# Where layer two's softmax denominators are summed: a stage of their own, or inside pass two

## The chip, the cores and the metric

The program runs on one core of a Trainium2 chip. The metric is the device time of the slowest (here the only) core, in microseconds. The kernel before takes 3942.93 us, the median of 3 runs (3939.38 to 3952.08).

## What is computed

A graph of 3125 nodes with 256 features and 103,125 edges (50,000 drawn ones in both directions and one loop per node, sorted by destination) goes through two layers. The first is attention with 8 heads, then a projection and a two-layer MLP with norms. The second, which this change touches, is

```python
z = proj_s[src] + proj_t[dst]
z = jnp.where(z >= 0, z, NEG_SLOPE * z)
e = (z @ W_attn.T)[:, 0]
m = jax.ops.segment_max(e, src, num_segments=n)
e_exp = jnp.exp(e - m[src])
denom = jax.ops.segment_sum(e_exp, src, num_segments=n)
alpha = e_exp / denom[src]
msg = feature[src] * alpha[:, None]
agg = jax.ops.segment_sum(msg, dst, num_segments=n)
return agg @ W_fc.T + b_fc
```

The maximum is taken by source node and the denominator is summed by source node, while the edges lie in order of destination. All scores here lie within 60 of each other, so one shift common to all edges does instead of one per node; a slow path behind a test holds for other data, and isn't taken.

## The kernel before

Edges lie in tiles of 128 (one edge per partition); there are 806 tiles (`T`), and a visit takes `G` = 30 of them, so that 27 visits walk over all. Each pass over the edges is a loop over the visits, written out separately for each engine, with semaphores between the engines.

- Pass one is the attention of layer one. GpSimd gathers the rows of the source nodes by index (line 779, two gathers of 128 rows for each of the 15 pairs of tiles), TensorE expands the rows of the destination nodes with one-hots (line 900), VectorE multiplies and reduces, TensorE sums by node (line 913).
- A stage by nodes (projection, MLP, norms) writes `proj_rows`, `narrow_rows` and `part_rows` to DRAM.
- Pass two computes the scores `e`. For each pair p of a visit, GpSimd gathers `proj_rows` or `narrow_rows` into the one slot of that pair, as soon as VectorE has read the pair of the visit before (`slots_free[1]`) and the indices are there (`idx_in[1]`). TensorE expands the pair into `px` (line 900; it runs up to 3 pairs ahead), VectorE adds both (`rows`, line 1615) and takes the dot product with the attention vector (`attend`, lines 1620 and 1622). At the visit's end three small instructions (lines 1633, 1635, 1638) put 30 columns of scores into `e_all`. ScalarE makes the one-hots of the destination nodes for the visit to come (lines 1142, 1147). SyncE sends the gathered features on to `x_edges` in the order of the edges (lines 545, 546) and loads indices and one-hot sources.
- After pass two come the range of the scores (lines 1646 to 1656), one exponential over `e_all` on ScalarE (line 1286), and then the denominators: `e_exp` is split into three bf16 parts (lines 1702, 1705), and for each of 26 blocks of `DT` = 31 tiles VectorE builds one-hots of the high part of the source (`src` // 128, 25 values; line 1715) and of its low part (`src` % 128; line 1716), multiplies the high ones by the three parts (line 1719), and TensorE runs 31 matmuls of 75 columns that add into `pn` (line 1045). Low and high one-hots are double-buffered. VectorE then sums the three parts (line 1722), takes reciprocals (lines 1725 to 1736), scales the node features by them (line 1743, 5 pieces), and SyncE writes these as `feat_rows` (line 725).
- Before line 1698 VectorE waits for `x1_back`, one load of all node features (line 684). SyncE holds the loads of low parts (line 691), of the streams `x_edges` (line 687) and of the first output row back until `recip2`, the last step of the reciprocals.
- Pass three gathers `feat_rows` (GpSimd waits for all of `feat_stored`), weighs them by `e_exp` and the looked-up reciprocals, and sums by destination node.

## Time and profile before

| | us |
|---|---|
| median of 3 runs | 3942.93 |
| span of the profiled execution | 3995.8 |
| pass one | about 150 to 1560 |
| stage by nodes | about 1560 to 1910 |
| pass two | 1907 (first gather) to 3173.7 (last scores) |
| range and exponential | 3173.7 to 3183.9 |
| denominators | 3183.9 to 3309 |
| scaled features, first loads | 3309 to 3333 |
| pass three | 3333 to 3996 |

The profile is one execution; of its own time only the span, from the first to the last instruction, is recorded, and it lies 52.9 us above the median of the runs. How to read it: the page gives the busy share of each engine over the whole span, and 40 slices of it. A table by stretch gives the same for parts. Groups put instructions of one line and shape together with their mean duration and with the engine's idle time just before them, and name what ended that idle time. The timeline shows single instructions.

### The profile page before, as it was taken

What the parts mean: (1) busy time and instruction counts of PE and PEld (TensorE: products, weight loads), DVE (VectorE), ACT (ScalarE), POOL (GpSimd) and SP (SyncE); (2) the same over time, 40 slices, a digit from 0 to 9 for tenths busy, and PEclk for the clock granted to TensorE, in tenths of its full rate; (3) what the DMA queues carried; (4) which work ended last, traced back from release to release, by engine and by line L of the source; (5) the groups of instructions that cost most, each with busy time, mean ns of one, the idle gap of its engine ahead of it and who ended that gap; (6) DMA issues with size and microseconds to landing.
All of it is one profiled execution on the core that took longest, in us unless ns stands there. A gap on an engine that the chain in (4) does not pass through costs nothing.

```text
span 3995.8 us, 54572 instructions
## 1 busy us (share of the span) xinstructions
PE 2303.1 (58%) x11454; PEld 1677.2 (42%) x11455; DVE 2175.4 (54%) x6197; ACT 1124.8 (28%) x2699; POOL 1960.5 (49%) x1970
## 2 busy tenths in 40 slices
PE   4456666666666664878233333333334395777776
PEld 2244444444444443756122222222122294656655
DVE  5455655556555564242344444444444596677676
ACT  0144554445544553333111111111112100111111
POOL 0255555555555553121566666666656303544443
PEclk9788877788778877988666666667666656988898
DMA  4666656666666663121677777777767505666564
GB/s 141 195 179 178 182 176 180 175 180 181 177 178 176 176 177 100 50 86 47 191 215 221 212 211 214 211 214 228 210 206 216 175 0 186 205 197 204 183 208 150
DMA packets 365707, 698.62 MB, mean 175 GB/s; under 512 B 77317, under 2 KB 247039, under 8 KB 365674
## 3 DMA queue, kind: packets, MB, share of 16 engines
q0 software_dynamic: 134784, 425.63, 36.1%
q1 hardware_dynamic: 220602, 256.40, 20.6%
q10 hardware_dynamic: 10288, 16.23, 1.1%
q8 instruction: 10, 0.16, 0.0%
q14 instruction: 23, 0.19, 0.0%
HBM read 597.23 MB, written 100.85 MB: 175 GB/s over the span
## 4 chain that ended last, share of the span: by engine, by line
another core or an unknown queue 27%; PE 26%; DVE 24%; issue 16%; DMA 3%; DVEq 2%; SPq 1%; POOL 1%; ACT 1%; ACTq 0%; POOLq 0%
PE ps_px L900 7%; DVE sb_prod L1622 4%; DVE sb_wide L1615 4%; DVE sb_score L1468 4%; PE ps_pa L913 3%; PE ps_px L913 2%; PE ps_px L998 2%; PE ps_px L1007 2%; PE ps_pa L1058 2%; PE ps_pn L1045 2%; DVE sb_wide L1477 1%; PE ps_px L876 1%; DVE sb_parts L1814 1%; DVE sb_prod L1462 1%
## 5 line engine op out<-in xcount | busy, mean ns | idle before, releaser
L900 PE MATMUL ps_px<-sb_parts 128*128 x2430 | 468.2, 358 | 798.8 <-DVE sb_wide L1615 563.1
L900 PEld LDWEIGHTS ps_px<-sb_parts 128*128 128x128 bf16 x2430 | 268.1, 122 | 999.4 <-DVE sb_wide L1615 625.6
L779 POOL DMA_INDIRECT sb_ring<-kv_rows,sb_idx x324 | 322.5, 995 | 357.8 <-DVE sb_wide L1477 152.6
L913 PE MATMUL ps_pa<-sb_wide,sb_onehot 128*128 128x264 f32 x864 | 302.8, 483 | 317.1 <-DVE sb_wide L1477 256.2
L779 POOL DMA_INDIRECT sb_ring<-proj_rows,sb_idx x324 | 316.5, 977 | 303.8 <-issue 170.8
L779 POOL DMA_INDIRECT sb_parts<-kv_rows,sb_idx x324 | 316.0, 975 | 206.9 <-DVE sb_wide L1477 107.4
L1142 ACT ACTIVATE sb_parts<-sb_bits,sb_nn_tab 128x768 bf16<-128x768 int16 x135 | 126.3, 937 | 1016.6 <-remote 606.9
L900 PE MATMUL ps_px<-sb_parts,sb_xwm 128*128 x2430 | 397.9, 309 | 19.2 <-ACT sb_xwm L1147 14.6
L779 POOL DMA_INDIRECT sb_w<-narrow_rows,sb_idx x324 | 315.3, 973 | 163.7 <-issue 102.2
L913 PE MATMUL ps_px<-sb_wide,sb_onehot 128*128 128x264 f32 x756 | 252.9, 466 | 197.3 <-DVE sb_wide L1477 124.3
L779 POOL DMA_INDIRECT sb_w<-feat_rows,sb_idx x162 | 158.9, 981 | 416.0 <-issue 192.3
L913 PEld LDWEIGHTS ps_pa<-sb_wide,sb_onehot 128*128 128x128 f32 x864 | 187.2, 239 | 371.1 <-DVE sb_wide L1477 258.6
L900 PEld LDWEIGHTS ps_px<-sb_parts,sb_xwm 128*128 128x128 bf16 x2430 | 270.6, 111 | 149.3 <-issue 51.1
L1622 DVE SCALAR_TENSOR_TENSOR sb_prod<-sb_wide,sb_attn_hi 128x256 f32<-128x256 f32 x810 | 310.5, 422 | 0.0
L1161 ACT ACTIVATE sb_onehot<-sb_bits 128x256 f32<-128x256 bf16 x405 | 166.3, 411 | 469.8 <-remote 316.7
L1154 ACT ACTIVATE sb_bits<-sb_iota_w,sb_ndst_f 128x128 bf16<-128x128 f32 x810 | 278.8, 391 | 40.7 <-issue 28.2
L1615 DVE TENSOR_TENSOR sb_wide<-ps_px,sb_ring 128x516 f32<-128x516 f32 x162 | 111.2, 694 | 303.0 <-remote 221.7
L1468 DVE TENSOR_REDUCE sb_score<-sb_prod 128x16 f32<-128x512 f32 x405 | 273.8, 676 | 0.0
L913 PEld LDWEIGHTS ps_px<-sb_wide,sb_onehot 128*128 128x128 f32 x756 | 156.9, 228 | 242.1 <-DVE sb_wide L1477 115.1
L1615 DVE TENSOR_TENSOR sb_wide<-ps_px,sb_w 128x516 f32<-128x516 f32 x162 | 112.2, 693 | 237.2 <-remote 190.4
L1462 DVE TENSOR_TENSOR sb_prod<-ps_px,sb_ring 128x512 f32<-128x512 f32 x162 | 111.1, 686 | 232.0 <-remote 138.4
L1814 DVE TENSOR_SCALAR sb_parts<-sb_iota_n,sb_dst_g,sb_ex_g 128x128 f32<-128x128 f32 x810 | 218.4, 361 | 35.0 <-issue 33.7
(256 smaller groups left out, 4473.2 us busy)
## 6 DMA issues: line engine op xcount, KB each, us to landing
sb_bits<-dst_short SPq DMA_DIRECT2D x280, 192.0 KB
x_edges<-sb_ring SPq DMA_DIRECT2D x54, 768.0 KB
sb_slots<-x_edges SPq DMA_DIRECT2D x54, 768.0 KB
x_edges<-sb_slots SPq DMA_DIRECT2D x27, 768.0 KB
sb_w<-x_edges SPq DMA_DIRECT2D x27, 768.0 KB
sb_msg<-lo_rows SPq DMA_DIRECT2D x28, 576.0 KB
kv_rows<-sb_slots ACTq DMA_DIRECT2D x25, 256.0 KB, 2.8
sb_parts<-part_rows SPq DMA_DIRECT2D x28, 193.5 KB
```

What stands on the lines that cost most here:

```text
L779: pool.indirect_dma_start(out=out[:, i, :], out_offset=None, in_=rows, in_offset=bass.IndirectOffsetOnAxis(ap=idx[:, 2 * p + i:2 * p + i + ...
L900: mm = pe.matmul(into, hots_t[L][:, 2 * p + i, :], flat(visit_parts[:, bass.ds(parity, 1), a, 0:width]), start=(a == 0), stop=(a == 2))
L913: mm = pe.matmul(into[:, 0:C + H], onehot[:, j, :], sums_in[:, 2 * (p % FLIGHT) + i, :], start=(p % EARLY == 0 and i == 0), stop=True, ski ...
L998: mm = pe.matmul(px[:, 2 * (s % 2) + f // 4, (f % 4) * P:(f % 4 + 1) * P], w1[:, c, f * P:(f + 1) * P], tr[:, s, c, :], start=(c == 0), st ...
L1142: act.activation(hots_t[L][:, half(h), :], drow[:, h], ACT.Abs, bias=nn_tab[:, bass.ds(v, 1)]).then_inc(far[L], 1)
L1154: ins = act.activation(away[:, j, :], iota_w[:], ACT.Abs, bias=ndst_f[:, bass.ds(t0 + (2 * p + i), 1)])
L1161: act.activation(onehot[:, places(p), :], away[:, places(p), :], ACT.Relu, bias=1.0, scale=-1.0).then_inc(hot[0], 1)
L1462: dve.tensor_tensor(prod[:, p % 3].rearrange("p (j c) -> p j c", j=2), px[:, p % FLIGHT, :].rearrange("p (j c) -> p j c", j=2), kv_pairs[p ...
L1468: dve.tensor_reduce(score[:, p % FLIGHT], prod[:, p % 3].rearrange("p (j h d) -> p j h d", j=2, h=H), AX, ALU.add).then_inc(red1, 1)
L1615: dve.tensor_tensor(zbuf[:, pair(p), :], px[:, places(p), 0:CW], proj_slots(p)[:, :, 0:CW], ALU.add).then_inc(slots_free[1], 1)
L1622: ins = dve.scalar_tensor_tensor(out=prod[:, p % 3, i * C:i * C + C], in0=zbuf[:, 2 * (p % FLIGHT) + i, 0:C], scalar=0.0, in1=attn_hi[:], ...
L1814: ins = dve.tensor_scalar(weights[:, j, :], iota_n[:], dst_g[:, j:j + 1], ex_g[:, j:j + 1], ALU.is_equal, ALU.mult)
```

## The change

The denominators move into pass two. The exponential used for them is shifted not by the maximum over all edges but by the largest score of the first visit, which is found once, in the second visit. For each visit v, its 30 columns are handled during visit v+1: ScalarE takes the exponential of the 30 columns, VectorE splits it into three bf16 parts, makes the low one-hots of 30 tiles with one comparison (3840 columns), the high ones with one (750), and the product with the three parts (2250); TensorE runs 30 matmuls of 75 columns, 6 behind each of the pairs 10 to 14. The buffers are single now. The visit's last columns follow after the loop. The exponential over `e_all` stays (pass three needs it). The feature load comes back in 5 pieces, each waited for by the piece that it feeds; the loads of low parts and of the first output row don't wait any more, the streams wait for `den0`, and the scaled features come behind the first one-hots of pass three. The slow path sums its denominators by itself.

```diff
+            def top_transposed():
+                pe.wait_ge(shift_set, 1)
+                pe.transpose(pa[0:1, 0:P], top[:, 0:1], ident[:]).then_inc(shift_pe, 1)
...
+            def denominators(v, g):
+                if g == 0:
+                    pe.wait_ge(dv, v + 1)
+                for j in range(g * R, (g + 1) * R):
+                    mm = pe.matmul(pn[:, 0:3 * W], lo_hot[:, :, j], hi_ex[:, :, :, j].rearrange("p a n -> p (a n)"),
+                                   start=False, stop=True, skip_group_check=True)
+                mm.then_inc(dpe, 1)
...
+            def scored(v, earlier=None, second=False):
                 parity = visit_value(pe, "parity", v)
                 for p in range(PAIRS):
                     expand(1, CW, parity, v, p)
+                    if second and p == 2:
+                        top_transposed()
+                    if second and p == 4:
+                        top_spread()
+                    if earlier is not None and p >= PAIRS - HALVES:
+                        denominators(earlier, p - (PAIRS - HALVES))
...
+            def score_exps(v):
+                act.wait_ge(zs, v * len(ZS) + ZS["masked"])
+                act.wait_ge(shift_set, 3)
+                act.activation(ex_v, dots[:, 2], ACT.Exp, bias=shift[:, 0:1]).then_inc(den_ex, 1)
+
+            node_half(0)
+            with act.Fori(0, total - 1) as u:
+                node_half(act.snap(u + 1))
+                score_exps(u)
+            score_exps(last_visit(act))
...
+            dve.wait_ge(part_out, 2 * (W // NB) * 16 + 1)
+            dve.tensor_copy(low_iota, iota_b[:].unsqueeze(2).broadcast_to([P, P, G]))
+            dve.tensor_copy(iota_j, iota_b[:, 0:W].unsqueeze(2).broadcast_to([P, W, G])).then_inc(fv, 1)
...
+                if step == "high":
+                    dve.tensor_tensor(hi_hot, iota_j, src_hib[:, bass.ds(t0, G)].unsqueeze(1).broadcast_to([P, W, G]), ALU.is_equal).then_inc(dh, 1)
...
+                if step == "ex":
+                    dve.wait_ge(den_ex, v + 1)
+                    dve.tensor_tensor(left0, ex_v, kept, ALU.mult).then_inc(dsplit, 1)
...
+                if step == "low":
+                    t0 = visit_value(dve, "tile", v)
+                    dve.wait_ge(dpe, v * HALVES + HALVES)
+                    dve.tensor_tensor(lo_hot, low_iota, src_lob[:, bass.ds(t0, G)].unsqueeze(1).broadcast_to([P, P, G]), ALU.is_equal)
+                if step == "spread":
+                    done("part2")
+                    dve.wait_ge(dh, v + 1)
+                    dve.tensor_tensor(hi_ex, hi_hot.unsqueeze(1).broadcast_to([P, 3, W, G]),
+                                      ex_parts.unsqueeze(2).broadcast_to([P, 3, W, G]), ALU.mult).then_inc(dv, 1)
+
+            WEIGHED = {1: ["low"], 3: ["ex"], 4: ["part0"], 5: ["left1"], 6: ["part1", "high"], 7: ["left2", "part2", "spread"]}
...
+                    if earlier is not None:
+                        for step in WEIGHED.get(p, []):
+                            weighed(earlier, step)
...
+                dve.tensor_copy(kept, low_dots[:, 1]).then_inc(zs, 1)
...
-            dve.wait_ge(ea, 1)
-            dve.wait_ge(x1_back, 16)
-
-            dve.tensor_copy(iota_j, iota_b[:].unsqueeze(2).broadcast_to([P, P, DT])).then_inc(fv, 1)
...
-            with dve.Fori(0, TD // DT // 2) as it:
-                for b in range(2):
...
-                    dve.tensor_tensor(hi_hot[:, b], iota_j[:, 0:W], src_hib[:, bass.ds(t0, DT)].unsqueeze(1).broadcast_to([P, W, DT]), ALU.is_equal).then_inc(dh, 1)
-                    dve.tensor_tensor(lo_hot[:, b], iota_j, src_lob[:, bass.ds(t0, DT)].unsqueeze(1).broadcast_to([P, P, DT]), ALU.is_equal)
...
+            for step in ("low", "high", "ex", "part0", "left1", "part1", "left2", "part2", "spread"):
+                weighed(last, step)
...
             for c in (0, 1):
                 indices(tile, c)
-            sp.wait_ge(fv, FVS["recip2"])
             low_rows(tile)
+            features(0)
+            sp.wait_ge(fv, FVS["den0"])
             for c in range(THIRDS):
                 stream(tile, c)
-            features(0)
```

## Rows read from the trace of the kernel before

**Rows 1.** The page: span, busy time and share of each engine
```profile
span 3995.8 us, 54572 instructions
PE 2303.1 (58%) x11454; PEld 1677.2 (42%) x11455; DVE 2175.4 (54%) x6197; ACT 1124.8 (28%) x2699; POOL 1960.5 (49%) x1970
```

**Rows 2.** Table by stretch: bounds and length in us, then busy time per engine
```profile
core 0: us, PE busy (x) PEld busy (x) DVE busy (x) ACT busy (x) POOL busy (x), PEclk, DMA share, GB/s
150.00:1560.00 1410.00, 885.29 (x4252) 652.26 (x4253) 813.83 (x1803) 696.13 (x1970) 798.49 (x810) 0.80 0.61 177
1910.00:3152.00 1242.00, 456.78 (x2358) 260.86 (x2358) 560.39 (x2418) 218.33 (x261) 784.84 (x809) 0.63 0.71 214
3184.00:3309.00 125.00, 109.91 (x806) 105.83 (x806) 113.83 (x93) 0.00 (x0) 0.00 (x0) 0.50 0.00 0
```

**Rows 3.** Groups, 3183.5 to 3309 us: busy, mean ns, idle before, releaser
```profile
L1045 PE MATMUL ps_pn<-sb_parts 128*128 128x75 bf16 x806 | 109.9, 311 | 17.0 <-DVE sb_parts L1719 17.0
L1716 DVE TENSOR_TENSOR sb_parts<-sb_parts,sb_src_lob 128x3968 bf16<-128x3968 bf16 x26 | 59.4, 2286 | 0.0
L1719 DVE TENSOR_TENSOR sb_parts<-sb_parts,sb_msg 128x2325 bf16<-128x2325 bf16 x26 | 36.5, 1405 | 0.0
L1715 DVE TENSOR_TENSOR sb_parts<-sb_parts,sb_src_hib 128x775 bf16<-128x775 bf16 x26 | 15.0, 578 | 6.3 <-PE ps_pn L1045 5.8 <-DVEq L1708 0.5
```

**Rows 4.** Timeline, end of pass two: start, duration, engine, line, [idle before <-releaser]
```profile
3171.54 0.39 SPq L684 DMA_DIRECT2D sb_ring<-proj_rows  x1
...
3173.54 0.19 DVE L1638 TENSOR_TENSOR sb_e_all<-sb_e_all,sb_dots 128x30 f32 x1
...
3178.29 1.04 ACT L1286 ACTIVATE sb_e_all<-sb_e_all,sb_shift 128x896 f32<-128x896 f32 x1 [33.60 <-DVEq L1692]
...
3183.86 2.23 DVE L1698 COPY sb_parts<-sb_iota_b 128x3968 bf16<-128x3968 bf16 x1 [6.33 <-DMA sb_ring<-proj_rows]
```

**Rows 5.** Timeline, from the denominators to the first gather of pass three
```profile
3309.22 0.19 DVE L1740 COPY sb_hn<-sb_iota_b 128x75 bf16<-128x75 bf16 x1
...
3309.32 7.09 DVE L1743 TENSOR_TENSOR sb_ring<-sb_ring,sb_denom 128x1280 f32<-128x1280 f32 x5
...
3316.73 0.82 DVE L1749 TENSOR_SCALAR sb_bits<-sb_msg,sb_hn 128x2304 bf16<-128x2304 bf16 x1
3317.48 1.70 DVE L1756 TENSOR_TENSOR sb_bits<-sb_hn,sb_src_hib 128x450 bf16<-128x450 bf16 x3
...
3318.47 6.62 SPq L725 DMA_DIRECT2D feat_rows<-sb_ring  x5
...
3333.11 1.19 POOL L779 DMA_INDIRECT sb_w<-feat_rows,sb_idx  x1 [156.00 <-issue]
```

**Rows 6.** Gathers of line 779, two groups: min/median/max ns, first and last start
```profile
L779 POOL DMA_INDIRECT sb_slots<-kv_rows,sb_idx x162: 943/949/1286, 167.7 to 1515.1; - x162
L779 POOL DMA_INDIRECT sb_slots<-proj_rows,sb_idx x162: 945/949/1190, 1938.4 to 3148.9; - x162
```

**Rows 7.** Timeline of VectorE inside one visit of pass two
```profile
2523.60 0.70 DVE L1615 TENSOR_TENSOR sb_wide<-ps_px,sb_ring 128x516 f32<-128x516 f32 x1 [6.66 <-remote]
...
2536.28 0.70 DVE L1615 TENSOR_TENSOR sb_wide<-ps_px,sb_w 128x516 f32<-128x516 f32 x1 [11.23 <-remote]
```

**Rows 8.** Timeline of TensorE in the same visit
```profile
2516.24 0.84 PE L900 MATMUL ps_px<-sb_parts 128*128 x6 [0.53 <-issue]
...
2524.35 1.48 PE L900 MATMUL ps_px<-sb_parts 128*128 x6 [7.28 <-DVE sb_wide L1615]
```

**Rows 9.** Timeline of GpSimd in the same visit, its two long waits
```profile
2510.66 0.94 POOL L779 DMA_INDIRECT sb_ring<-proj_rows,sb_idx  x1 [5.90 <-DVE sb_wide L1615]
...
2537.79 0.94 POOL L779 DMA_INDIRECT sb_w<-narrow_rows,sb_idx  x1 [4.76 <-DVE sb_wide L1615]
```

**Rows 10.** Timeline, pass three: a gather and the VectorE instructions beside it
```profile
3396.25 2.01 POOL L779 DMA_INDIRECT sb_w<-feat_rows,sb_idx  x1 [0.30 <-issue]
```

**Rows 11.** Timeline of VectorE in the stretch of rows 10
```profile
3395.73 1.71 DVE L1756 TENSOR_TENSOR sb_bits<-sb_hn,sb_src_hib 128x450 bf16<-128x450 bf16 x3
```

More of the change, by code:

```diff
@@ L331, in build @@
         x_in = [sem(f"x_in{c}") for c in range(THIRDS)]
-        x1_back = sem("x1_back")
+        x1_back = [sem(f"x1_back{i}") for i in range(NB)]
+        shift_pe = sem("shift_pe")
+        shift_set = sem("shift_set")
+        den_ex = sem("den_ex")
         lo_in = sem("lo_in")
@@ L466, in build @@
         SPLITS = 5
+        ZS = steps(["dots", "low", "masked", "kept", "added"])
+        DS = steps(["ex", "part0", "left1", "part1", "left2", "part2"])
         feats = ring
@@ L683, in _ @@
             sp.sem_inc(sp_seen, 1)
-            sp.dma_start(x1, proj_rows[:, CW:ROW].rearrange("(w p) c -> p w c", p=P)).then_inc(x1_back, 16)
+            for i in range(NB):
+                some = slice(i * W // NB, (i + 1) * W // NB)
+                sp.dma_start(x1[:, some], proj_rows[i * W // NB * P:(i + 1) * W // NB * P, CW:ROW].rearrange("(w p) c -> p w c", p=P)).then_inc(x1_back[i], 16)
             def stream(tile, c):
@@ L1643, in _ @@
+            scored(0)
+            scored(1, 0, second=True)
+            with dve.Fori(0, total - 2) as u:
+                scored(dve.snap(u + 2), dve.snap(u + 1))
             for c in range(THIRDS):
@@ L1654, in _ @@
             dve.tensor_scalar(slow_i[:], dots[0:1, 1, 0:1], SPREAD, None, ALU.is_gt).then_inc(ev, 1)
-            dve.tensor_scalar(shift[:], rng_all[:, 0:1], -1.0, None, ALU.mult).then_inc(ev, 1)
-            dve.wait_ge(ev, 5)
+            dve.wait_ge(ev, 4)
+            dve.wait_ge(fv, FVS["dsum"])
             dve.sem_inc(slow_flag, 1)
@@ L1740, in _ @@
             dve.tensor_copy(hi_iota, iota_b[:, 0:W].unsqueeze(1).broadcast_to([P, 3, W])).then_inc(fv, 1)
-            for i in range(NB):
-                some = slice(i * W // NB, (i + 1) * W // NB)
-                dve.tensor_tensor(feats[:, some, :], x1[:, some, :], denom[:, 2, some].unsqueeze(2).broadcast_to([P, W // NB, C]), ALU.mult).then_inc(fv, 1)
             dve.wait_ge(fv, FVS["hi"])
+            dve.wait_ge(ea, 1)
             def low_onehots(v):
@@ L1837, in _ @@
             high_onehots(0)
+            for i in range(NB):
+                some = slice(i * W // NB, (i + 1) * W // NB)
+                dve.wait_ge(x1_back[i], 16)
+                dve.tensor_tensor(feats[:, some, :], x1[:, some, :], denom[:, 2, some].unsqueeze(2).broadcast_to([P, W // NB, C]), ALU.mult).then_inc(fv, 1)
             reciprocals(0)
```

173 lines of the change are left out of this document (106 added, 67 removed).

## The prediction

> **What bounds the kernel now.** I read the page first for the shares. No engine is over 58% busy [rows 1], so no engine bounds the whole, and each stage has to be read by itself. The table by stretch comes next, for the three stages that matter [rows 2]. In 3184 to 3309 TensorE is busy 109.9 of 125 us and VectorE 113.8, while GpSimd and the DMA stand still: a stage of engine work and nothing else. The groups of that stretch show its beat: per block of 31 tiles VectorE needs 0.58 + 2.29 + 1.41 = 4.27 us (lines 1715, 1716, 1719), and TensorE's 806 matmuls (26 blocks) are busy 109.9 us, 4.2 us per block [rows 3]. The two take turns with two buffers and cost about 4.7 us per block, 122 us for 26.
>
> Pass two, where this work is to go, is another matter. VectorE is busy 560 of 1242 us, TensorE 457, GpSimd 785 [rows 2]. The period of a visit comes from the first and last start of the gathers into the third room of slots: (3148.9 - 1938.4 - 6.3) / 26 = 46.3 us, where 6.3 are the five issues between the first and the last of a visit [rows 6]. 30 gathers at 1.25 us (0.95 busy, 0.30 between) are 37.6 us of it. So GpSimd is nearest to being the bound, and what it lacks, 8.7 us per visit, are a few waits. The timeline of one visit shows two long ones, 5.90 and 4.76 us, both ended by VectorE's line 1615, which frees the slots [rows 9]. And what does VectorE wait for? It idles 6.66 and 11.23 us before two pairs [rows 7], and the releaser is "remote", none that the trace knows. TensorE had started the pairs that VectorE needs long before: it is up to three pairs ahead, and its last starts are at 2516.24 and 2524.35 [rows 8]. I read it so: while GpSimd issues gathers, TensorE's completions reach VectorE late, and when GpSimd runs out of free slots and stops, they come all at once. VectorE works in bursts, one behind each stop, two stops per visit, and in a burst it has no idle time at all. The 25 us per visit in which VectorE is idle are thus not simply free: work put into a burst makes the burst longer.
>
> **The part that is removed.** The last scores of pass two are written at 3173.5 to 3173.7 and the first gather of pass three starts at 3333.1 [rows 4, 5]: 159.4 us. What stands there afterwards, step by step from 3173.7:
> - VectorE, last visit's columns: low one-hots 2.29 x 3840/3968 = 2.2 us, high ones 0.58 x 750/775 = 0.56, product 1.41 x 2250/2325 = 1.36 [rows 3], six small ones at 0.19 (the 30-column line 1638, [rows 4]) 1.1, two loads of the tile number and the wait before them, together about 1.3: 6.6 us, to 3180.3.
> - TensorE, 30 matmuls at 109.9/806 = 0.136 us [rows 3]: 4.1 us, to 3184.4. The range of the scores is taken beside them.
> - the sum of the parts and the test for the slow path 1.5 us, the reciprocals 2.0 as before, to 3187.9. The exponential over all scores, 1.04 us [rows 4], lies beside them.
> - first one-hots of pass three, 0.82 + 1.70, now ahead of the scaled features, 7.09 [rows 5]: to 3197.5.
> - stores. Before, 6784 KB (by shape: twice 576 low parts, 2304 streams, 128 output row, 3200 features) went between 3309.9 and 3333.1 [rows 5], 291 KB per us. Behind `den0` (3186.1) there are now 6080 KB, 20.9 us: the first gather at 3207.
>
> The feature load, which held VectorE until 3183.86 [rows 4], is hidden: its first user comes at 3190. Gain: 3333.1 - 3207 = 126 us. Bounds: 119 if VectorE's front counts (features done at 3316.4 before, 3197.5 after), 129 if the stores end with the last feature; I take the gathers' front, since pass three starts with it.
>
> **What is added to pass two.** Ahead of the first pair VectorE waits until the last `part_rows` are stored and copies the two index tables, 2.23 x 3840/3968 [rows 4] and about 0.5: 0 to 3 us, I take 3, for the first gather has landed by then. The common shift costs a transpose, a small matmul and three small instructions once: 1 us. ScalarE's exponential of 30 columns waits for the end of VectorE's visit; behind it on ScalarE stand the destination one-hots of the visit after the next, which can't start before TensorE has expanded the next visit's first three pairs anyway: nothing. TensorE's 30 matmuls are 4.1 us per visit on an engine with 17 of 46 busy, behind pairs 10 to 14, and it waits there for `dv`, which VectorE sets after pair 7; the pairs 8 to 10 are expanded by then: nothing as long as VectorE isn't later than that. SyncE's queue has nothing new inside the pass.
>
> VectorE gets per visit 2.2 + 0.56 + 1.36 + 7 x 0.19 = 5.5 us of work and about 0.4 us of register loads: 5.9, in 26 visits. None of it waits for TensorE's pairs, but all stands in pairs 1 to 7, in the first burst. Two prices follow.
> - More stops. 21.6 us of VectorE work per visit (560/26, [rows 2]) take two stops, 10.8 each; 27.5 us take 2.55. A stop costs GpSimd 4.76 less the usual 0.30, 4.5 us [rows 9]. 0.55 x 4.5 = 2.5 us per visit, 64 us. Bounds: 0 (it all fits where VectorE waits anyway) and a whole stop, 4.5 us per visit, 117 us. Pass one is a second reading of the same slope: its VectorE is busy 813.8/27 = 30.1 us per visit and its period is (1515.1 - 167.7 - 6.3)/26 = 51.6 us [rows 2, 6], 5.3 us more for 8.5 us more work, 0.62 per us, which would make 5.9 us cost 3.7. It has twice the TensorE work too, so I stay nearer to pass two's own figure.
> - Gathers held up. Beside three bf16 comparisons of VectorE with two inputs in SBUF (line 1756, 1.71 us together) a gather took 2.01 us instead of 0.95 [rows 10, 11]: 1.06 us lost of the 1.18 that they shared. The three added large instructions are of this kind. The low one-hots follow pair 1, about when GpSimd waits (until 2510.66, [rows 9]); high ones and product, 1.92 us, follow pairs 6 and 7, where it issues in 37.6 of 46.3 us: 1.5 us per visit, 40 us. Bounds 0 and 4.1 us, 107 us.
>
> The Trainium skill, SBUF — State Buffer, section "Who interferes with whom", speaks the other way: `tensor_tensor` has no two-port mode and takes only the read interface of the pair that VectorE shares with GpSimd, while writing descriptors needs the write interface (inferred, it says). By that the second price would be nothing and the sum 40 us lower. The trace disagrees: the gather of 2.01 us lay beside `tensor_tensor` alone.
>
> **Sum.** -126 + 3 + 1 + 64 + 40 = -18 us on the profiled execution. Its span is 52.9 us above the median of the runs, and I carry the difference over unchanged: 3942.9 - 18 = 3925 us.
>
> **Rivals.**
> 1. Slower: each visit takes one whole stop more, because the burst that would have handled pairs 0 to 8 ends at 5 or 6 and the second can't reach 14. For it: a burst has no idle time, and the largest addition (low one-hots) stands at its start. Against it: some completions do arrive while GpSimd issues (2523.60, [rows 7]). Price 4.5 + 1.5 = 6.0 us per visit, 156 us: -126 + 4 + 156 = +34, 3977 us. It turns the sign once a visit grows by more than (126 - 4)/26 = 4.7 us.
> 2. No gather is held up, the stops as forecast: -58, 3885 us. For it: GpSimd's long waits may lie over the large instructions. Against it: rows 10.
> 3. All is hidden, because VectorE is idle 25 us per visit: -122, 3821 us. Against it: those waits end with GpSimd's stops, not with time.
> 4. It doesn't do what it says: the stage goes, but features or stores take its place. The order above shows nothing later than 3207, so I give it no time of its own; it lies inside rival 1's side.
>
> **How the numbers follow.** Forecast 0.45 (its own range 3895 to 3960), rival 1 with 4: 0.30, rival 2: 0.13, rival 3: 0.12. A measurement of this kernel tells about 0.3%, 12 us, from no change. Faster than that: rivals 2 and 3 and 0.25 of the forecast, 0.50; within it 0.14; slower: rival 1 and 0.06 of the forecast, 0.36. The range leaves out rival 3 and the upper end of rival 1, where both prices reach their bounds: 3850 to 4000.
>
> **What would show it.** Right: the stretch without DMA behind pass two shrinks from 125 us to under 15; the first gather of pass three starts 30 to 37 us after the last scores; the gathers' starts give a period of 49 to 51.5 us for pass two, with more than two long GpSimd waits in many visits; some gathers of pass two take 1.5 to 3 us beside the new instructions. Wrong: a period of 46 to 47 us (rival 3; 48.8 for rival 2) or over 51.5 (rival 1); TensorE waiting long for `dv`, or VectorE for the exponential, would be waits that I priced at nothing.

## The result and the profile after

| | before | after |
|---|---|---|
| median of 4 runs, us | 3947.51 (3939.38 to 3955.39) | 3837.42 (3827.48 to 3838.77) |
| span of the profiled execution | 3995.8 | 3825.7 |

The ratio is 0.9722, 95% interval 0.9698 to 0.9746: 110 us less, where 18 were forecast (3942.9 to 3925), and 13 us below the range. The two profiled spans differ by 170 us. 60 us of that are no work of the change: the execution of before lay 48 us above the median of the four runs, and that of after 12 below its own. Part of these 60 can be seen in pass one, whose code is the same: it took 51.6 us per visit in the profiled execution of before and 50.2 in that of after, some 35 us in sum.

The page of the kernel after, span and busy time, against [rows 1]:

```profile
span 3825.7 us, 55082 instructions
PE 2265.8 (59%) x11461; PEld 1680.5 (44%) x11462; DVE 2190.3 (57%) x6388; ACT 1162.1 (30%) x2751; POOL 2033.0 (53%) x1970
```

The table by stretch (length, busy time of each engine, granted clock, DMA share, GB/s), against [rows 2]: pass one, pass two, and 34 us behind the last scores, where the stage of 125 us without any DMA stood:

```profile
150.00:1560.00 1410.00, 894.47 (x4264) 653.01 (x4264) 817.40 (x1823) 695.48 (x1974) 804.02 (x814) 0.80 0.62 178
1910.00:3152.00 1242.00, 535.81 (x3201) 376.57 (x3201) 706.28 (x2771) 257.12 (x311) 831.70 (x780) 0.66 0.72 213
3131.00:3165.00 34.00, 9.53 (x58) 8.31 (x59) 27.35 (x62) 2.37 (x3) 0.86 (x2) 0.51 0.86 298
```

The groups of VectorE in 1910 to 3152 (count, busy, mean ns, idle before), against [rows 3]:

```profile
L1683 DVE TENSOR_TENSOR sb_parts<-sb_parts,sb_src_lob 128x3840 bf16<-128x3840 bf16 x27 | 58.1, 2151 | 2.3 <-issue 2.3
L1687 DVE TENSOR_TENSOR sb_parts<-sb_parts 128x2250 bf16<-128x2250 bf16 x27 | 35.9, 1331 | 0.9
L1668 DVE TENSOR_TENSOR sb_parts<-sb_parts,sb_src_hib 128x750 bf16<-128x750 bf16 x27 | 14.5, 537 | 0.0
```

The timeline from the last scores to the first gather of pass three, against [rows 4, 5]:

```profile
3130.91 0.19 DVE L1738 TENSOR_TENSOR sb_e_all<-sb_e_all,sb_dots 128x30 f32 x1
...
3133.37 2.16 DVE L1683 TENSOR_TENSOR sb_parts<-sb_parts,sb_src_lob 128x3840 bf16<-128x3840 bf16 x1 [2.27 <-issue]
...
3142.99 0.24 DVE L1760 TENSOR_REDUCE sb_dsum<-ps_pn 128x25 f32<-128x75 f32 x1 [2.41 <-PE ps_pn L1052]
...
3147.98 1.70 DVE L1853 TENSOR_TENSOR sb_bits<-sb_hn,sb_src_hib 128x450 bf16<-128x450 bf16 x3
...
3149.60 7.09 DVE L1938 TENSOR_TENSOR sb_ring<-sb_ring,sb_denom 128x1280 f32<-128x1280 f32 x5
3151.11 5.97 SPq L739 DMA_DIRECT2D feat_rows<-sb_ring  x5
...
3164.52 1.19 POOL L793 DMA_INDIRECT sb_w<-feat_rows,sb_idx  x1 [23.42 <-issue]
```

From the end of the last scores, 3131.1, to the first gather of pass three, 3164.5, are 33.4 us. The kernel before took 159.4 and the prediction put 33.3 there. This part is right: 126 us.

Pass two, then, is where the forecast's other 108 us should have been lost. The gathers of line 793 into the third room of slots, with their first and last start, against [rows 6]:

```profile
L793 POOL DMA_INDIRECT sb_slots<-proj_rows,sb_idx x162: 941/947/1168, 1901.5 to 3101.3; - x162
```

(3101.3 - 1901.5 - 6.3)/26 = 45.9 us per visit, 46.3 before. The 5.9 us of VectorE work that each visit received cost nothing in sum. This is the period that the prediction had named as the sign of its rival 3. That is not because nothing happened. The three groups of gathers of pass two (busy, mean ns | idle before, by what ended it), first of before, then of after:

```profile
L779 POOL DMA_INDIRECT sb_ring<-proj_rows,sb_idx x324 | 316.5, 977 | 303.8 <-issue 170.8 <-DVE sb_wide L1615 108.0 <-DMA sb_idx<-in_src 25.0
L779 POOL DMA_INDIRECT sb_w<-narrow_rows,sb_idx x324 | 315.3, 973 | 163.7 <-issue 102.2 <-DVE sb_wide L1615 61.5
L779 POOL DMA_INDIRECT sb_slots<-proj_rows,sb_idx x162 | 155.8, 962 | 55.7 <-issue 48.2 <-DVE sb_wide L1615 7.6
```

```profile
L793 POOL DMA_INDIRECT sb_ring<-proj_rows,sb_idx x324 | 360.5, 1113 | 281.8 <-issue 164.1 <-DVE sb_wide L1699 101.9 <-DMA sb_idx<-in_src 15.8
L793 POOL DMA_INDIRECT sb_w<-narrow_rows,sb_idx x324 | 348.7, 1076 | 101.0 <-issue 97.5 <-DVE sb_wide L1699 3.5
L793 POOL DMA_INDIRECT sb_slots<-proj_rows,sb_idx x162 | 153.9, 950 | 52.5 <-issue 49.2 <-DVE sb_wide L1699 3.3
```

An undisturbed gather takes 0.947 us, so 810 of them 767.1. Before, the three groups sum to 787.6, after to 863.1: the gathers were held up for 20 us before and 96 after, 75 us more. And the idle time that isn't "issue", GpSimd's stops, sums to 202 us before and 124 after, 78 us less. The two cancel.

One visit of after shows how. GpSimd, VectorE and TensorE, three timelines, against [rows 9, 7, 8]:

```profile
2503.85 0.95 POOL L793 DMA_INDIRECT sb_slots<-proj_rows,sb_idx  x1 [0.30 <-issue]
2509.70 1.03 POOL L793 DMA_INDIRECT sb_ring<-proj_rows,sb_idx  x1 [4.91 <-DVE sb_wide L1699]
2512.30 1.89 POOL L793 DMA_INDIRECT sb_ring<-proj_rows,sb_idx  x1 [1.56 <-issue]
...
2522.84 2.06 POOL L793 DMA_INDIRECT sb_w<-narrow_rows,sb_idx  x1 [0.30 <-issue]
```

```profile
2507.88 1.29 DVE L1699 TENSOR_TENSOR sb_wide<-ps_px,sb_ring 128x516 f32<-128x516 f32 x2 [13.96 <-remote]
...
2511.21 2.15 DVE L1683 TENSOR_TENSOR sb_parts<-sb_parts,sb_src_lob 128x3840 bf16<-128x3840 bf16 x1
...
2555.09 1.30 DVE L1699 TENSOR_TENSOR sb_wide<-ps_px,sb_ring 128x516 f32<-128x516 f32 x2 [18.15 <-remote]
```

```profile
2508.63 4.05 PE L916 MATMUL ps_px<-sb_parts 128*128 x18 [15.56 <-DVE sb_wide L1699]
...
2524.14 1.00 PE L1052 MATMUL ps_pn<-sb_parts 128*128 128x75 bf16 x6 [3.53 <-DVE sb_parts L1687]
...
2534.59 0.84 PE L916 MATMUL ps_px<-sb_parts 128*128 x6 [0.47 <-DVE sb_wide L1699]
```

There is one stop (4.91 us, ahead of a visit's first gather) where there were two. VectorE works in one piece from 2507.88 to 2536.9, through all fifteen pairs and the denominators (busy 26.0 of the 29 us, no pause over 1.8), and then waits 18.15 us for a completion of pairs that TensorE had started by 2534.59. The gathers of 1.89 and 2.06 us lie beside lines 1683 and 1687.

The instruction of line 1699 needs two things, the pair from TensorE and the landing of the gather, so a late landing is a rival to a late completion. The trace also keeps the times at which semaphores changed, and they decide it. TensorE's matmuls for the three pairs that VectorE then takes up ended at 2533.5, 2534.1 and 2535.4, by the profile's model of their ends; the semaphore that they raise (`expd[1]`) changed at 2554.95, 2555.03 and 2555.11. The landing increments of the first pair's gathers that the trace has stand at 2515.0 to 2518.3. In all of pass two, 49 of the 52 gaps of over 2 us before line 1699 (445 of 477 us) end within 0.25 us of such a change. It is not simply that completions are late while gathers are issued: from 2510 to 2534 TensorE finished twelve more pairs while GpSimd issued all the time; of the ten changes recorded for them six stand within 0.1 us of the end of a pair's matmuls, and the last is 1.8 us late.

### The profile page after: what moved, and what is told of

It reads as the page before. It is cut to its first block, busy times and chain, and to the rows that moved or that the text cites. A ratio compares the mean times of both kernels' runs of the same rounds, so it can differ in the third digit from the quotient of the medians.

```text
span 3825.7 us, 55082 instructions
## 1 busy us (share of the span) xinstructions
PE 2265.8 (59%) x11461; PEld 1680.5 (44%) x11462; DVE 2190.3 (57%) x6388; ACT 1162.1 (30%) x2751; POOL 2033.0 (53%) x1970
## 4 chain that ended last, share of the span: by engine, by line
PE 31%; another core or an unknown queue 23%; DVE 21%; issue 16%; DMA 3%; DVEq 2%; SPq 2%; ACT 1%; POOL 1%; ACTq 0%; POOLq 0%
PE ps_px L916 10%; DVE sb_score L1517 4%; PE ps_pa L929 3%; PE ps_px L929 3%; DVE sb_prod L1706 3%; PE ps_pn L1052 3%; PE ps_px L1014 2%; DVE sb_wide L1699 2%; PE ps_px L1023 2%; PE ps_pa L1093 2%; DVE sb_wide L1526 1%; PE ps_px L892 1%; DVE sb_prod L1511 1%; DVE sb_parts L1911 1%
## 5 line engine op out<-in xcount | busy, mean ns | idle before, releaser
L916 PE MATMUL ps_px<-sb_parts 128*128 x2430 | 457.1, 349 | 609.8 <-DVE sb_wide L1699 465.4
L916 PEld LDWEIGHTS ps_px<-sb_parts 128*128 128x128 bf16 x2430 | 276.8, 121 | 757.2 <-DVE sb_wide L1699 490.7
L793 POOL DMA_INDIRECT sb_ring<-proj_rows,sb_idx x324 | 360.5, 1113 | 281.8 <-issue 164.1
L793 POOL DMA_INDIRECT sb_w<-narrow_rows,sb_idx x324 | 348.7, 1076 | 101.0 <-issue 97.5
L1511 DVE TENSOR_TENSOR sb_prod<-ps_px,sb_parts 128x512 f32<-128x512 f32 x162 | 110.8, 684 | 208.5 <-remote 145.4
```

The lines of the kernel that those rows point to most:

```text
L793: pool.indirect_dma_start(out=out[:, i, :], out_offset=None, in_=rows, in_offset=bass.IndirectOffsetOnAxis(ap=idx[:, 2 * p + i:2 * p + i + ...
L916: mm = pe.matmul(into, hots_t[L][:, 2 * p + i, :], flat(visit_parts[:, bass.ds(parity, 1), a, 0:width]), start=(a == 0), stop=(a == 2))
L1511: dve.tensor_tensor(prod[:, p % 3].rearrange("p (j c) -> p j c", j=2), px[:, p % FLIGHT, :].rearrange("p (j c) -> p j c", j=2), kv_pairs[p ...
```

## The experiments

All are edits of the kernel after. The sets of runs were taken on different chips and at different times, and each ratio is to the kernel before of its own set, whose median stands with the set. Sets B and D have no run of the kernel after; their ratios are set beside those of sets A, C, E and F, which is a weaker comparison. Two sets, D and F, are a case of their own, below. A stop is a pause of GpSimd for want of a free slot. "Held up" is the time of a visit's gathers over 0.95 us each, "waits" the pauses between them over 0.30 us, both means of 24 visits of pass two, in us per visit; 37.5 + held up + waits is the period.

| set (before, us) | kernel | ratio to before, 95% | pass two, first to last gather | held up | waits |
|---|---|---|---|---|---|
| A (3947.5) | before | 1 | 1242.0 | 0.7 | 8.3 |
| A | after | 0.9722 (0.9698 to 0.9746) | 1232.2 | 3.7 | 4.8 |
| B (4025.1) | e1_large_cut | 0.9739 (0.9706 to 0.9772) | 1272.1 | 1.0 | 9.1 |
| B | e2_low_three_times | 0.9877 (0.9854 to 0.9899) | 1315.9 | 5.9 | 5.9 |
| B | e3_other_instruction | 0.9766 (0.9727 to 0.9805) | 1281.7 | 5.0 | 5.5 |
| B | e4_small_matmul_behind | 0.9813 (0.9764 to 0.9863) | 1289.6 | 3.6 | 7.1 |
| C (4017.1) | control (after) | 0.9727 (0.9664 to 0.9789) | 1246.6 | 3.9 | 5.2 |
| C | e5_one_input_in_psum | 0.9899 (0.9835 to 0.9963) | 1313.3 | 0.8 | 10.8 |
| C | e6_all_ahead_of_first_pair | 1.0021 (0.9986 to 1.0056) | 1368.0 | 1.1 | 12.7 |
| C | e7_one_matmul_of_six | 0.9649 (0.9591 to 0.9708) | 1240.6 | 3.6 | 5.2 |
| D (3277.9) | e8_gpsimd_drains_once | 0.9962 (0.9941 to 0.9983) | 1152.4 | 2.7 | 2.6 |
| D | e9_gpsimd_drains_half | 0.9885 (0.9854 to 0.9915) | 1128.3 | 3.4 | 0.9 |
| D | e10_psum_and_pauses | 0.9639 (0.9614 to 0.9663) | 1037.2 | 0.8 | 0.1 |
| E (3933.0) | control_b (after) | 0.9743 (0.9710 to 0.9777) | 1225.6 | 3.9 | 4.3 |
| E | e8_drains_once_b | 0.9718 (0.9665 to 0.9771) | 1232.5 | 3.9 | 4.7 |
| E | e9_drains_half_b | 0.9683 (0.9642 to 0.9724) | 1223.4 | 3.7 | 4.4 |
| E | e11_psum_and_half_drains | 0.9830 (0.9796 to 0.9864) | 1274.8 | 0.7 | 9.4 |
| F (3273.2) | control_c (after) | 0.9773 (0.9758 to 0.9788) | 1091.6 | 2.9 | 0.1 |
| F | e12_drains_once_at_11 | 1.0167 (1.0147 to 1.0187) | 1215.2 | 2.3 | 5.3 |
| F | e13_drains_half_at_11 | 0.9765 (0.9751 to 0.9779) | 1090.6 | 2.8 | 0.2 |

The expectations name their theories by letters. B: the period is GpSimd's issue time with the held-up gathers, plus one stop. C: something else sets it. D: a stop begins where VectorE has caught up with TensorE. E: completions get through when gathers pause. F: a completion is seen only once another instruction has followed on TensorE. G: completions are late whatever follows.

### The added work taken away, and tripled

e1_large_cut:

```diff
-dve.tensor_tensor(lo_hot, low_iota, src_lob[...]..broadcast_to([P, P, G]), ALU.is_equal)
+dve.tensor_tensor(lo_hot[:, 0:1], low_iota[:, 0:1], src_lob[...]..broadcast_to([P, 1, G]), ALU.is_equal)
```

and the same for the high one-hots and the product; the three buffers are filled with ones once, ahead of the pass.

> The three large VectorE instructions of each visit (low one-hots 3840 columns, high ones 750, product 2250) handle 30 or 90 columns only, so the denominators are not those of the reference; all else stays, TensorE's 30 matmuls too. VectorE has 4.0 us per visit less. Forecast's theory (the period of a visit grows with VectorE's work, by stops and held-up gathers): 3.2 us per visit less, 83 us, about 3755 us. Theory B (the period is GpSimd's issue time, held-up gathers included, plus one stop): the held-up time goes, 60 us by the gathers beside the three instructions, about 3777 us, unless the second stop of the kernel before comes back, which gives it all back. Theory C (something else sets 46 us per visit): 3837 us within 12.

Measured: 0.9739, the ratio of the change itself within its interval. With 2.7 us of held-up time less per visit, the waits are 9.1 us instead of 4.8 to 5.2: the second stop is back. Neither the forecast's theory (83 us less) nor B's 60 holds; what B named as its exception happened. Work that costs about 0 when added gives about 0 when taken away, but the two halves of that 0 are large: over 27 visits some 73 us of held-up time less and 105 to 116 us of waits more.

e2_low_three_times repeats the comparison twice more, each waiting for the one before it.

> The low one-hots are made three times over per visit: 4.3 us more VectorE work of the kind that held gathers up. Forecast's theory: 1.8 us per visit for stops and 3 for gathers, 4.8 x 26 = +125 us, about 3960 us. Theory B: only the held-up gathers, 1.15 us for each comparison, 2.3 x 26 = +60 us, about 3897 us. Theory C: 3837 us within 12; period 46 us.

Measured: 0.9877, 1.3 to 1.6% of the kernel before above the change (sets A, C and E), 54 to 62 us: theory B's 60, half of the forecast's 125. Gathers are held up 2.0 to 2.2 us more per visit and the waits don't fall (5.9 us against 4.3 to 5.2). There was only one stop left, and this one did not go: here more held-up time is a plain cost.

### The same results by other instructions

e3_other_instruction:

```diff
-dve.tensor_tensor(lo_hot, low_iota, src_lob[...], ALU.is_equal)
+dve.scalar_tensor_tensor(out=lo_hot, in0=low_iota, scalar=0.0, in1=src_lob[...], op0=ALU.add, op1=ALU.is_equal)
```

and likewise for the other two (the product in three pieces).

> The same three results by scalar_tensor_tensor instead of tensor_tensor, which should take about 1.1 ns a column instead of 0.56, so 3.5 us more VectorE work per visit, and may not hold gathers up. Forecast's theory: the slope of VectorE's work costs 1.5 us per visit, the gathers give 1.5 to 2.3 back: within 25 us of 3837. Theory B: held-up gathers gone, up to 60 us less, about 3780 us; if gathers beside it still take 1.6 us and more, no gain. Theory C: 3837 us within 12.

e5_one_input_in_psum:

```diff
+dve.tensor_copy(pa[:, C:C + G], src_lob[:, bass.ds(t0, G)]).then_inc(in_bank, 1)
+dve.wait_ge(in_bank, v * 3 + 1)
-dve.tensor_tensor(lo_hot, low_iota, src_lob[...]..broadcast_to([P, P, G]), ALU.is_equal)
+dve.tensor_tensor(lo_hot, low_iota, pa[:, C:C + G].unsqueeze(1).broadcast_to([P, P, G]), ALU.is_equal)
```

> The small operand of each of the three large instructions (30, 30, 90 columns) is first copied to PSUM, so that they have one input in SBUF: about 1.15 ns a column by the 1350-column instruction of pass three with one input in PSUM (1.56 us), beside which gathers weren't held up: 3.4 us more VectorE work per visit and three small copies of 0.2 us. Forecast's theory (VectorE's work costs stops): 4 us more per visit cost 1.7, gathers give 2.3 back: within 20 us of the changed kernel. Theory B or D (period is 30 issues of 1.25 us, the held-up time and one stop): the held-up time falls by 2.3 us per visit, 60 us less than the changed kernel, ratio to before about 0.957.

Measured: 0.9766 for e3 (0.4% above the control, inside the intervals), 0.9899 for e5: 64 us slower than the control beside it instead of 60 faster. These two are the pair to compare, for the large instructions take VectorE the same time in both. The low one-hots in the groups of VectorE, 1910 to 3190, first e3, then e5:

```profile
L1684 DVE SCALAR_TENSOR_TENSOR sb_parts<-sb_parts,sb_src_lob 128x3840 bf16<-128x3840 bf16 x25 | 103.9, 4156 | 2.3 <-issue 2.3
```

```profile
L1690 DVE TENSOR_TENSOR sb_parts<-sb_parts,ps_pa 128x3840 bf16<-128x3840 bf16 x25 | 103.8, 4154 | 0.9
```

and the three groups of gathers, first e3, then e5:

```profile
L793 POOL DMA_INDIRECT sb_ring<-proj_rows,sb_idx x324 | 402.6, 1243 | 202.0 <-issue 161.3 <-DVE sb_wide L1703 34.7 <-DMA sb_idx<-in_src 5.9
L793 POOL DMA_INDIRECT sb_w<-narrow_rows,sb_idx x324 | 339.0, 1046 | 100.0 <-issue 97.7 <-DVE sb_wide L1703 2.4
L793 POOL DMA_INDIRECT sb_slots<-proj_rows,sb_idx x162 | 153.7, 949 | 153.5 <-DVE sb_wide L1703 111.0 <-issue 42.5
```

```profile
L794 POOL DMA_INDIRECT sb_ring<-proj_rows,sb_idx x324 | 313.2, 967 | 306.0 <-issue 152.8 <-DVE sb_wide L1709 112.5 <-DMA sb_idx<-in_src 21.9
L794 POOL DMA_INDIRECT sb_w<-narrow_rows,sb_idx x324 | 320.4, 989 | 170.3 <-issue 85.1 <-DVE sb_wide L1709 84.6 <-remote 0.6
L794 POOL DMA_INDIRECT sb_slots<-proj_rows,sb_idx x162 | 158.6, 979 | 111.2 <-DVE sb_wide L1709 63.3 <-issue 47.9
```

The instruction takes 4.16 us in both, and stands behind the same pair. In e3 both inputs are in SBUF and the gathers sum to 895 us, 128 held up; in e5 one input is in PSUM and they sum to 792, 25 held up. The stops are the other way round: 154 us in e3, 283 in e5.

The pair is not clean, though. e5 has three small copies more, and VectorE waits for its own increment behind each of them. In its trace one of these waits is long. It is the high one-hots' line, in the same view:

```profile
L1674 DVE TENSOR_TENSOR sb_parts<-sb_parts,ps_pa 128x750 bf16<-128x750 bf16 x24 | 22.4, 935 | 57.1 <-remote 49.1 <-issue 7.6
```

The longest: a copy ended at 2346.88 and the semaphore that it raises changed at 2355.15, 8.3 us later, on the engine that waited for it. So increments of VectorE itself come late too, not only TensorE's. This is a second reason for stops in e5. It isn't the main one: of the 24 visits, the 14 in which VectorE did not wait there have 9.4 us of stops each, the other 10 have 12.5, and e3, counted alike, has 5.4. So the amount of VectorE's large work and its place did not by themselves take the second stop away. It goes where gathers are held up, and returns where they aren't, here as in e1.

### The work moved, and TensorE's part

e6_all_ahead_of_first_pair:

```diff
+if earlier is not None and not second:
+    for step in ("low", "high", "ex", "part0", "left1", "part1", "left2", "part2", "spread"):
+        weighed(earlier, step)
 rows(0)
...
-if earlier is not None:
+if second:
     for step in WEIGHED.get(p, []):
         weighed(earlier, step)
```

> All nine steps of the denominators stand ahead of VectorE's first pair of the visit instead of behind pairs 1 to 7; the same instructions. Theory D (a stop begins where VectorE has caught up with TensorE; work between pairs 1 and 7 lets TensorE stay ahead, which removed the stop at pairs 7 to 10): the second stop comes back, 3.5 us per visit, 90 us more than the changed kernel, ratio 0.995. Theory B (only the amount of work counts, and the held-up gathers): as the changed kernel, within 15 us. Forecast's theory: as the changed kernel or up to a stop worse.

Measured: 1.0021, 117 us more than the control: the same instructions cost the whole gain of the change when they stand there. The number came out near theory D's 90, but e3 and e5 speak against its reason. GpSimd stands still at this place, waiting for the first pair, so the large instructions hold no gather up (1.1 us per visit), they lengthen the stop instead (7.4 us ahead of the first gather, 5.0 in the control), and the stops further on, 5.3 us in sum, are those of a kernel with no gather held up.

e7_one_matmul_of_six:

```diff
-for j in range(g * R, (g + 1) * R):
+for j in range(g * R, g * R + 1):
```

> TensorE runs one matmul of the six of each group, 5 instead of 30 per visit, so the denominators are sums over a sixth of the tiles. Forecast priced TensorE's matmuls at nothing: within 12 us of the changed kernel. Theory D: TensorE is 3 us faster in pairs 10 to 14 and stays ahead; the 0.2 of a long stop per visit that the changed kernel has over one goes: 0 to 20 us less.

Measured: 0.9649, 28 us below the control. The intervals to the kernel before overlap, but they share its scatter; taken directly, all four runs of e7 (3870 to 3890 us) lie below all four of the control (3894 to 3914). In the traces pass two is 6 us shorter and its tail 4 us. So TensorE's matmuls, which the prediction priced at nothing, probably cost something, 10 us by the traces and 28 by the medians; where the rest arises the runs don't show.

e4_small_matmul_behind puts a matmul of one column behind each pair that TensorE expands:

```diff
 mm.then_inc(expd[L], 1)
+if L:
+    pe.matmul(pn[:, 3 * W:3 * W + 1], zeros[:, 0:P], zeros[:, P:P + 1], start=True, stop=True, skip_group_check=True)
```

(it writes to the bank in which the denominators are summed, and its denominators are not the reference's.)

> Behind each pair that TensorE expands in pass two stands one more matmul of one column into an unused column. Theory F (a completion of TensorE is seen only once another instruction has followed it, and in the changed kernel the last pairs ahead, at 2533.86 and 2535.16, stay unseen for 20 us for that reason): VectorE's wait of 14 us before a visit's first pair and GpSimd's stop of 4.9 us go, period 41 to 42 us, about 3725 us. Theory G (completions are late while gathers are issued, whatever follows): VectorE's wait stays, 3837 to 3850 us.

Measured: 0.9813, 0.7 to 0.9% of the kernel before above the change, waits of 7.1 us, and VectorE idles 524 us in gaps of over 2 us, 477 in the kernel after. Theory F falls: a completion is not late for want of a next instruction on TensorE. The time itself says less, for the edit has a side effect: between 1910 and 3150 us TensorE is busy 818 us instead of the control's 522, at a granted clock of 0.54 instead of 0.66.

### Pauses made by GpSimd itself

e8 and e9 wait once per visit, ahead of pair 10, until the gathers of pair 9 (e8) or of pair 8 (e9) have landed:

```diff
+if p == 10:
+    landed(pool, 1, total, v, p - 1)
 slot_free(1, v, p)
```

> The changed kernel; once per visit, ahead of pair 10, GpSimd waits until its gathers of pair 9 have landed, so that none is in flight. Theory E (TensorE's completions get through when gathers pause): at that point VectorE sees the first pairs of the next visit, 13 us earlier than now, and the stop of 5 us at GpSimd's first pair goes; it costs a pause of 3 us: 2 us per visit less, 55 us less than the changed kernel, ratio to before about 0.958. Rival (the stop at the first pair is needed for another reason): 3 us per visit more, 78 us more, ratio 0.992.

> The same, but the wait is for pair 8, with the two gathers of pair 9 still in flight. Theory E, if a thinner stream of gathers is enough: pause of 1 to 2 us instead of the stop of 5, 3 us per visit, 80 us less, ratio about 0.952. If only an empty queue lets completions through: no stop saved, 1 to 2 us per visit more, ratio 0.979 to 0.986.

e10 adds 16 semaphore increments ahead of the pairs 1 and 4 to e5's edit:

> The kernel with the small operands in PSUM (no gather held up, 10.8 us of stops per visit), and GpSimd pauses by itself: 16 semaphore increments of some 0.07 us ahead of pair 1 and of pair 4, 2.2 us per visit. Theory E (held-up gathers are pauses in which completions get through): the second stop goes again, 10.8 falls to about 5.5 us, in sum 3 us per visit less than without the pauses, about 3890 us where that kernel takes 3968. Rival (the held-up gathers were only a cost, and the instruction's place or length decides): 2.2 us per visit more, about 4025 us.

These three fell into set D, where something else was to be seen, below; there GpSimd had no stops that a pause could have saved, and e8 and e9 show only what a pause costs (2.6 and 0.9 us per visit). In e10 the increments left no pause at all between the gathers (waits 0.1 us), so e10 is e5's edit and nothing more. The test was made again:

> The changed kernel, unaltered, beside the three runs of this chip. On a chip whose kernel before takes about 4000 us: ratio 0.972. On one like that of the last three runs (kernel before 3278 us, no late completion, GpSimd never stopped): pass two is 30 issues of 1.25 us and the held-up time, 37.5 + 3.5 = 41 us per visit, against 38.3 of the kernel before: 27 visits x 2.7 = 73 us lost of the 126 won at the end, ratio 0.98.

> The wait of GpSimd ahead of pair 10 until no gather is in flight, again, for a chip with late completions: theory E 55 us less than the changed kernel beside it (the stop at the first pair goes), the rival 78 us more. On a chip without them: 2.6 us per visit more, 60 us more.

> The wait with two gathers still in flight, again: theory E, if a thinner stream is enough, 80 us less than the changed kernel beside it; if only an empty queue helps, 20 to 50 us more. On a chip without late completions: 0.9 us per visit, 25 us more.

e11 waits ahead of the pairs 3, 6 and 10 for the pair two before, on top of e5's edit:

> Small operands in PSUM (no gather held up), and GpSimd waits ahead of the pairs 3, 6 and 10 until only the two gathers of the pair before are in flight, about 0.9 us each. On a chip with late completions, theory E (any thinning of the gathers lets completions through): the 10.8 us of stops that this kernel has without the waits fall to 5.5 with 2.7 of pauses, 65 us less than the 1.0175 of the changed kernel that it took without them: about that of the changed kernel. Rival (held-up gathers help in another way): 2.7 us per visit on top, 1.035 of the changed kernel. On a chip without late completions: 0.98 of the changed kernel or a little above.

Measured in set E: e8 and e9 at 0.9718 and 0.9683 against 0.9743 for the control, 17 us each, less than the intervals tell. In e8 the wait at pair 10 takes 2.7 us and the one ahead of the first gather falls from 3.8 to 1.1: the stop has moved, the sum has not changed (4.7 against 4.3). So a stop may stand elsewhere, but a full drain costs what it saves; the 55 us were wrong. e11 came out at 0.983, 1.009 of its control where e5 took 1.018 of its own. Its pauses at the three pairs take 4.5 us, the stops elsewhere fall from the 10.8 of e5, in another set, to 4.9: GpSimd's own pauses, too, take the place of stops, 4.5 us for 5.9. The held-up gathers do it at a better exchange, 3.1 us for 5.6 between e5 and its control. That e11 would reach the changed kernel's time was too hopeful by 35 us.

The last set asked the same one pair later:

> The changed kernel, unaltered, for comparison on this chip: 0.972 to 0.975 of the kernel before where completions come late (before 3930 to 4030 us); 0.98 on a chip like the one with 3278 us.

> GpSimd's wait for an empty queue one pair later than before, ahead of pair 11, when VectorE has surely ended its visit (it ended about at pair 10, and the wait there saved the stop at the first pair in only a part of the visits). Theory E: the stop at the first pair, 4.3 us, goes in nearly every visit and the wait costs 2.7: 1.6 us per visit, 40 us less than the changed kernel, 0.989 of it. Rival (a stop is needed once per visit in any case, wherever it stands, and costs the same): 1.000 of it within 0.005.

> The same wait with the last two gathers still in flight, 0.8 us. Theory E, if half is enough: 0.98 of the changed kernel. As seen at pair 10 (0.8 us of pause, 1.4 us of stop saved): 0.995. Rival: 1.005.

It fell under the conditions of set D again, so that its question stays open for those of the prediction; e12 shows a wait of 5.3 us per visit at its full price (4.0% over the control), e13 one that was already fulfilled when it was reached.

### Two sets in which no completion was late

In sets D and F the kernel before took 3273 to 3278 us instead of 3933 to 4025, and GpSimd had no stop in pass one or two (waits per visit in pass one 0.0 us, 11 to 13 in the other sets). What ended VectorE's waits before its first instruction on a pair (line 1699), first in the kernel after of set A, then in the same kernel in set F:

```profile
its engine sat idle before it (us, times) until:
  remote: 427.1, 46
  PE ps_px L916: 69.7, 55
```

```profile
its engine sat idle before it (us, times) until:
  DMA sb_w<-narrow_rows,sb_idx: 114.0, 67
  DMA sb_ring<-proj_rows,sb_idx: 112.8, 99
  DMA sb_slots<-proj_rows,sb_idx: 78.4, 73
```

In set A VectorE waits for completions that come from nowhere the profile knows, 9 us at a time, and takes up most pairs 30 to 44 us behind the start of their gather. In set F it waits for hardly anything but the landing of the gathers, and is 5 to 7 us behind them. The period there is GpSimd's issue and the held-up time, 37.5 + 2.9 = 40.4 us, and nothing pays for a held-up gather: e10, with the small operands in PSUM, takes 38.4 us per visit and has the largest relative gain of all, 0.9639 against 0.9773 for the control of set F (the two sets' kernels before differ by 0.14%): some 44 us, by pass two 54. This compares two sets. The same edit cost 64 us in set C.

## Why the prediction was right and wrong

The sign was right, with a chance of 0.50 for faster by over 0.3%; the time was outside the range, 13 us below it.

- **The removed stage, -126 us:** right. 33.4 us from the last scores to the first gather against 33.3 worked out. Inside, VectorE's last columns took 7.4 us instead of 6.6, and the features ended 25.6 us behind the last scores instead of 23.8; from there to the first gather it was 7.8 us instead of 9.5. That the two errors cancel to 0.1 us is luck.
- **The start of pass two, +3:** right as far as it can be seen: first gather to VectorE's first pair 12.4 us, 9.8 before. The prices of nothing mostly held, too: VectorE did not wait for ScalarE's exponential. It was wrong that TensorE wouldn't wait for `dv`: it idled 209.6 us before line 1052, until VectorE's line 1687. What that cost isn't settled: e7 has fewer matmuls but still has the wait.
- **More stops, +64 us:** this step failed, and by its sign. Stops fell by 78 us. I had taken 10.8 us of VectorE's work as what one stop buys, from 21.6 us of work and two stops per visit, and so made every added microsecond buy a part of another. (The 21.6 were themselves 0.7 too many, since the stretch of 1242 us holds 26.8 visits and not 26; that changes nothing.) The kernel after does 26 us of work in one piece. A stop does not come after so much work; it comes when completions stop reaching VectorE, and that depends on how freely the gathers run (e1, e3 against e5, and e11). I put the lower bound at 0 ("it all fits where VectorE waits anyway") without a reason that excluded a gain. The next term of my own sum, the held-up gathers, was what made one.
- **Gathers held up, +40 us:** the mechanism was right, the size by half too small: 75 us. The 26 low one-hots did not fall where GpSimd waits. That stop ends with VectorE's first pair, and the one-hots stand behind pair 1, by which time GpSimd is issuing again. The beat of the kernel after shows it, 2507.88, 2509.70, 2511.21. Worked out from all gathers of the control: those that overlap line 1683 take 1.62 us on average, line 1687 2.00, none of VectorE's work 0.945.

The Trainium skill, SBUF — State Buffer, "Who interferes with whom", infers that `tensor_tensor` takes only the read interface of the shared pair and leaves descriptor writing alone. The gathers of 1.89 and 2.06 us shown above, and the means just given, say that such gathers are held up all the same. The prediction quoted half of that section: it also says that a VectorE instruction with two SBUF inputs contends with a GpSimd instruction that reads SBUF. These gathers take their indices from SBUF (`sb_idx` in their rows), and by that rule the traces agree with the section. That it is the reading of the indices no run here separates. Of the same section, the statement that an instruction with at most one SBUF input and outside the two-port modes doesn't contend with GpSimd agrees with e5: beside its 4.15 us comparison a gather takes 0.968 us.

- **The rivals.** Rival 3 (all hidden, 3821) came nearest in time, with 0.12, and its sign, a period of 46 to 47 us, is the one that was nearly seen (45.9). But its reason is refuted: the work isn't hidden in idle time, it holds gathers up by 75 us, and the same work costs 117 us in e6. Rival 2 (no gather held up) is refuted by the rows of the gathers. Rival 1 (a whole stop more per visit, 3977) describes e6 well, 4021 of 4017, where the steps stand ahead of the first pair; it was the right fear for another place. Of the signs that the prediction named, the first gather 33.4 us behind the last scores and the gathers of 1.9 to 2.1 us came; the period of 49 to 51.5 us and the additional stops did not. Stops and held-up gathers were added as if independent. They are linked, and a sum of terms with one sign each could not give that. That the total is only 13 us outside the range is no merit of the sum: two of its terms are wrong by 142 us and 35 us in opposite directions.
- The 110 us of the medians are 126 less 5 for a longer last visit (last gather to last scores 29.8 us, 24.8 before) and about 11 in pass two and elsewhere, which the single traces (pass two 10 us shorter after the change) cannot resolve.

**What stays open.** Why increments reach VectorE late in some executions and not in others, and what it is in a held-up or paused gather that lets them through. No version was found that is better than the change under the conditions of the prediction by more than the intervals tell; e9 is 17 us below its control, unsettled. Under the conditions of sets D and F the edit of e5 is better by about 1.4%.

## What to carry to other kernels

Write down the period of the engine that issues (number of issues times their undisturbed time, held-up time, waits) and watch all three in every version: a term that grows may be what keeps another small, and a bound of a new cost must be argued on both sides of nothing. An instruction put beside gathers is priced by where the issuing engine is at that moment, not only by its length: the same nine steps cost next to nothing behind pairs 1 to 7 and 117 us more ahead of pair 0. Before an edit is tuned against stops that end with no known releaser, run it under more than one condition: here the edit that lost 64 us in one set won about 44 in another.

## What the runs showed of the hardware

- Semaphore increments can reach a waiting engine late: TensorE's reached VectorE 19 us late (raised at 2554.95, matmuls ended by 2535.4), and VectorE's own 8.3 us late (e5, 2346.88 to 2355.15). It was so in every profiled execution of four sets and in none of two. The chip number doesn't decide it: number 13 gave set C, 4017 us, and later set F, 3273. The kernel before takes 17 to 19% less time in the sets without it.
- SyncE is slow in the same stretches: in the gaps of VectorE of over 5 us in pass two, 107 of its 186 waiting or register-move instructions took 0.70 us in the kernel after, 34 of 714 outside them, and none of 912 in the control of set F. What the two have in common isn't known.
- A large bf16 VectorE instruction with both inputs in SBUF held gathers up whether it was tensor_tensor at 0.56 ns a column (2.15 us) or scalar_tensor_tensor at 1.08 ns (4.16 us); with one input in PSUM, at the same 1.08 ns a column, it did not. Beside the short f32 scalar_tensor_tensor of line 1622, with two inputs in SBUF too (256 columns, 0.42 us), a gather of the kernel before takes 1.00 us instead of 0.95.
- A wait of GpSimd for all of its last gathers takes 2.6 us ahead of pair 10 (e8) and 5.3 ahead of pair 11 (e12). With two gathers left in flight it takes 0.8 to 0.9 us ahead of pair 10 (e9), nothing ahead of pair 11 (e13), and 3.0 ahead of pair 3 (e11).
